# Maxima pieces around the two score steps of an attention block

## The reference

```
x = x + 0.5 * ffn(layernorm(x))     # router picks 1 of 8 experts per token: (u * silu(g)) @ w_down.T
x = x + attention(layernorm(x))
x = x + 0.5 * ffn(layernorm(x))     # the same weights again

attention: q = x @ Wq.T             # 8 heads of 64
           kv = x @ Wkv_down.T      # latent of 64, shared by the heads
           k, v = kv @ Wk_up.T, kv @ Wv_up.T
           out = softmax(q k.T / 8) v @ Wo.T
```

## Time and profile before

| | |
|---|---|
| time, median of 3 runs | 1205.15 us (1203.85 to 1205.66) |
| the profiled execution: its time | 1205.7 us |
| the profiled execution: span, first to last instruction | 1203.9 us |
| mean granted TensorE clock, as a share of 2.4 GHz | 0.92 |
| busy: PE, DVE, POOL, ACT | 984.3, 735.9, 676.9, 483.2 us |
| DVE's reductions L737 | 256, 311.9 us in sum |
| attention loop, pairs of heads | from about 240 us to 1020 us |

### The profile page before, as it was taken

The page is one execution under the profiler, slowest core; times in us unless marked ns, Lnnn a source line. Parts: engine busy times, 40 slices in busy tenths (PEclk is TensorE's granted clock), DMA queues, the critical chain, the costliest instruction groups (busy, mean ns, idle before and its releaser), DMA issues.

```text
span 1203.9 us, 17005 instructions
## 1 busy us (share of the span) xinstructions
PE 984.3 (82%) x5096; PEld 551.8 (46%) x5097; DVE 735.9 (61%) x1195; ACT 483.2 (40%) x760; POOL 676.9 (56%) x385
## 2 busy tenths in 40 slices
PE   5839975399999989999988999998999999469700
PEld 4828842144444454434454444445344555448600
DVE  6565556747677745667774677777566735555431
ACT  1253431154444434444434444442355653444300
POOL 0025452267868717768754777773587885045371
PEclk9999967599999989999999999999899999569955
DMA  8054532100000100000010000001002000145453
GB/s 292 0 171 149 146 95 91 39 1 1 1 2 1 62 1 1 1 1 1 1 62 2 1 1 1 1 1 62 1 1 106 2 1 1 63 144 162 131 151 120
DMA packets 40046, 62.22 MB, mean 52 GB/s; under 512 B 5936, under 2 KB 33072, under 8 KB 38960
## 3 DMA queue, kind: packets, MB, share of 16 engines
q1 hardware_dynamic: 20000, 27.40, 6.4%
q0 software_dynamic: 6912, 18.88, 5.8%
q10 hardware_dynamic: 13072, 15.09, 3.6%
HBM read 30.81 MB, written 23.07 MB: 45 GB/s over the span
## 4 chain that ended last, share of the span: by engine, by line
PE 63%; DVE 16%; issue 8%; ACT 5%; DMA 3%; POOL 1%; DVEq 1%; ACTq 0%; POOLq 0%; SPq 0%
PE ps_o L949 16%; PE ps L936 9%; PE ps L731 7%; PE ps L571 6%; DVE maxes L737 5%; DVE rows_store L1259 5%; PE ps_x L711 4%; PE ps L1082 3%; PE ps L208 2%; PE ps_x L970 2%; ACT rows_store L487 2%; PE ps L555 2%; PE ps_o L587 1%; PE ps_x L587 1%; PE ps L223 1%
## 5 line engine op out<-in xcount | busy, mean ns | idle before, releaser
L737 DVE TENSOR_REDUCE maxes<-ps 128x2 f32<-128x1024 f32 x256 | 311.9, 1218 | 213.9 <-PE ps L731 211.4
L1342 POOL TENSOR_TENSOR arena_b<-arena_b 128x1024 f32<-128x1024 f32 x112 | 268.3, 2396 | 164.1 <-PE ps_o L949 123.1
L1342 POOL TENSOR_TENSOR arena_b<-arena_b,hot_store 128x1024 f32<-128x1024 f32 x112 | 268.8, 2400 | 84.1 <-ACT hot_store L1140 42.1
L936 PE MATMUL ps<-q_split,keys_now 64*128 64x512 f32 x1536 | 207.2, 395 | 0.0
L1140 ACT ACTIVATE arena_b<-ps 128x1024 f32<-128x1024 f32 x144 | 144.4, 1023 | 104.3 <-PE ps L936 104.1
L520 POOL DMA_INDIRECT arena_b<-scaled_x,token_of x80 | 75.7, 947 | 179.3 <-issue 81.7
L936 PEld LDWEIGHTS ps<-q_split,keys_now 64*128 64x128 f32 x1536 | 147.5, 188 | 31.7 <-issue 2.4
L949 PE MATMUL ps_o<-arena_b,latent_now 128*64 128x512 f32 x576 | 148.9, 617 | 3.1 <-ACT arena_b L1140 0.4
L1140 ACT ACTIVATE hot_store<-ps 128x1024 f32<-128x1024 f32 x112 | 111.9, 1022 | 54.9 <-PE ps L936 54.7
L1259 DVE RECIPROCAL rows_store<-rows_store 128x256 f32<-128x256 f32 (+1 forms) x72 | 112.6, 1565 | 12.0 <-ACT rows_store L1151 12.0
L949 PE MATMUL ps_o<-hot_store,latent_now 128*64 128x512 f32 x448 | 116.6, 617 | 3.3 <-ACT hot_store L1140 0.9
(11 more groups left out here) (182 smaller groups left out, 1145.8 us busy)
## 6 DMA issues: line engine op xcount, KB each, us to landing
sorted_y<-arena_b ACTq DMA_DIRECT2D x80, 128.0 KB
scaled_x<-rows_store SPq DMA_DIRECT2D x32, 256.0 KB, 2.1
x_res<-x_in SPq DMA_DIRECT2D x4, 1024.0 KB, 13.0
keys_now<-keys_next SPq DMA_DIRECT2D x4, 1024.0 KB, 4.6
out<-x_res SPq DMA_DIRECT2D x32, 128.0 KB
arena_a<-w_gu SPq DMA_DIRECT2D x1, 2048.0 KB, 15.9
keys_max_now<-keys_max_next SPq DMA_DIRECT2D x4, 512.0 KB, 5.4
arena_a<-w_gu ACTq DMA_DIRECT2D x1, 2048.0 KB, 7.7
```

The source lines that it names most:

```text
L737: nc.vector.tensor_reduce(maxes[:, 2 * m:2 * m + 2], ps[2][:, :, :], AX_X, ALU.max) \
L936: last = nc.tensor.matmul(ps_s[n % 2][:, a, :], keys_now[h, key, k], query[h, p, q], start=False, stop=(kt >= KT - STRIDE and query is q_h ...
L1342: nc.gpsimd.tensor_tensor(t, t, prob(k, kt).rearrange("p a n -> p (a n)"), ALU.add) \
```

## The change

In a block the first piece stood ahead of both score steps, and the second behind both. Now the first stands between the two score steps. Nothing else changes: the same instructions, the same buffers.

```diff
                         after_values(p, d)
+                        scores(p, 2 * d)
                         piece()
-                        scores(p, 2 * d)
                         scores(p, 2 * d + 1)
                         piece()
```

## The result

The changed kernel takes 1265.06 us (median of 4 runs, 1264.38 to 1265.23), the kernel before beside it 1205.41 (4 runs): ratio 1.0495, 95% interval 1.0477 to 1.0514, 59.7 us slower. The forecast was 1265, +59.8. The profiled execution has a span of 1263.4, 59.5 more than before.

The account below looks back on a forecast made before the run. TensorE in program order was taken as the bound, with its waits for reductions and exponentials. Three looped batches (47.1) and the last batch (12.7) gave +59.8 us, forecast 1265 us; 8-in-10 range 1246 to 1284.

Parts of the forecast that it names:

- What holds a plain block: In plain blocks, the first piece's reduction keeps the second piece at least 1.82 us behind; the values wait for the exponential.
- the turning point: Plain block: at a reduction of 0.74 us, pieces 1.33 apart, values would start at 2.45 us, as before the change.
- The first rival: The reduction does not gate the second piece; values start 0.3 us earlier in some 90 blocks, 1178 us; chance 0.03.
- Cost of a plain block: A plain block goes from 4.37 to 4.86 us, +0.49, because the second piece waits for the reduction.
- a distance under 1.8: Declared sign of error: in a plain block the second piece comes under 1.8 us behind the first.
- The reciprocals' cover: Blocks behind a reciprocal: its delay is hidden with 0.03 us to spare, so they cost only 0.24 us each.
- Second blocks, key blocks, router blocks: Second blocks of a pair +0.69 us each, first blocks with key splits +0.92, last-batch blocks with router transposes +0.62.
- I take no change: TensorE's clock stays at the 2.4 GHz level although each longer block adds an idle 0.7 to 0.8 us.
- the second sign of being wrong: Declared sign of error: TensorE's granted clock inside the pairs falls below 0.99.
- the third rival: TensorE's clock falls in a tenth of the blocks, 12 x 3.0 = +36 us, 1301 us, open upwards; chance 0.06.
- the second rival: POOL's additions pace the last blocks of a pair, so its lag absorbs part of the loss: 1243 us; chance 0.07.
- the classes of the three looped batches: Losses by kind of block in the loop's 32 blocks per batch: 15.7 us a batch, 47.1 for three.

Follow-up runs that it names:

- experiments 1: Reductions reading 128 of 512 columns: kernel before 1174.87 us, changed kernel 1164.08 us; reading 256 columns in the changed kernel: 1188.48 us.
- experiment 2: Changed kernel with both pieces behind both score steps, nothing between the pieces: 1366.87 us, ratio 1.1332 to the kernel before.
- experiment 4: Half reciprocals cut in two around the first reduction: under the kernel before 1201.3 us (ratio 0.9974), under the changed kernel 1265.06 us (1.0503).
- experiment 3: Changed kernel with the first piece ahead of both score steps again in the six key blocks: 1252.11 us, ratio 1.0396 to the kernel before.

## Why the prediction was right

- *What holds a plain block* (two pieces apart by the reduction, values by the exponential): right, shown by experiments 1 and 2 from both sides, and for the turning point: 0.74 us was worked out, and with 0.69 the block is 4.28 against 4.37. The first rival, by which the reduction would not hold the second piece, is out.
- *Cost of a plain block*: 0.49 forecast, 0.44 measured. A piece that follows scores and not values is issued 0.80 behind the block's start, but runs 0.40 and not 0.50, and its reduction starts 0.43 to 0.45 behind it, not 0.54. So the pieces can be 1.72 apart; I had held 1.82 for their least distance, and had named a distance under 1.8 as a sign of being wrong. That sign came, and it is the hand-over that was mis-sized by 0.1, not the wait that was misread.
- *The reciprocals' cover*, called thin by 0.03: it held (experiment 4), 0.21 against 0.24 a block.
- *Second blocks, key blocks, router blocks*: 0.70, 0.93 to 0.96, 0.63 to 0.69, as worked out. Two blocks of a batch were put in a wrong class: the third of the first pair costs 0.63 and not 0.49, and the second of the last pair nothing where 0.24 was due.
- *The clock*: the step "I take no change" failed in places, and with it came the second sign of being wrong, a granted clock under 0.99 inside the pairs: it is 0.96 over each of the four with such a block (552 to 600, for one), and 1.00 from 503 to 549, in a pair without. In plain blocks the step holds (full clock with 0.65 idle in 4.83), but I did not ask it of the block with the longest wait, where two waits now stand close together. Three stretches are 1.6 above their class and one 1.15, with 0.5 more in the stretch ahead of that one: 6.5 us. That is the third rival in small, four blocks in place of twelve, at half its price. The old order in the key blocks brings the clock back (experiment 3), so the new order there is what brings the low clock about. The two waits are not the whole condition: the same ones left the clock alone in two blocks of the changed kernel, and longer ones in three of experiment 2, while the changed kernel with cut reciprocals fell in the same four as the changed one. What else it takes stays open. The Trainium skill ("TensorE: Matmul & The Clock Gate", A second HAM failure mode: psum-queue depth-cycling) says that frequent small idle times between matmul groups make the clock swing. In the plain blocks this trace does not agree (0.65 idle, clock 1.00); in the key blocks the clock does fall, though not each time.
- *POOL's lag* (the second rival): the last blocks of a pair cost 0.21 to 0.46 all the same, so they absorb none of it; what it gives back lies at the ends of the batches, as told next.

The total is closer than its parts, and that it came within 0.1 us is luck, because their errors offset each other: the classes of the three looped batches sum to 14.6 a batch and not 15.7 (-3.4), the last batch to 13.0 and not 12.7 (+0.3), the clock adds 6.5, and the stretches between two batches and ahead of the loop are 3.7 shorter than before (31.79, 30.38 and 24.86 became 30.24, 30.22 and 23.66, and 0.8 ahead). Together 47.1 - 3.4 + 13.0 + 6.5 - 3.7 = 59.5, the measured difference of the spans.

Why the stretches between batches are shorter can be read from the traces. Behind the last values of a batch the output product (L1082) waits for DVE's last multiplication L1266, before and after:

```profile
414.52 2.34 DVE L1266 TENSOR_TENSOR arena_b<-arena_b,rows_store 128x512 f32<-128x512 f32 x1
416.92 3.72 PE L1082 MATMUL ps<-w_vo,arena_b 128*128 128x256 f32 x16 [1.72 <-DVE arena_b L1266]
```

```profile
431.49 1.09 DVE L1266 TENSOR_TENSOR arena_b<-arena_b,rows_store 128x512 f32<-128x512 f32 x1
432.64 3.72 PE L1082 MATMUL ps<-w_vo,arena_b 128*128 128x256 f32 x16 [0.47 <-DVE arena_b L1266]
```

It starts 1.25 behind the values in both, but takes 1.09 in place of 2.34, and so TensorE waits 1.25 less, in each of the three places. What differs is POOL: the addition that L1266 meets there ends 3.05 behind the values before and 1.80 after, as if POOL had caught up in the longer blocks. In both kernels L1266 ends 0.55 behind the end of that addition, which fits a wait for it; no run varied POOL by itself. This gain is 3.75 in all, and the sum had no term for it. In the second of the three places 1.1 is lost again: the granted clock is low for 6.8 us there and not for 3.4. The 0.8 ahead of the loop wasn't followed up.

## What to carry to other kernels

Where one buffer is filled and drained in turn, look at the distance between the two fills in the in-order queue and compare it with fill, drain and hand-over; spreading the fills "evenly" over the work only helps if the smaller distance stays above that. A wait for something else (here the exponential) may hide that such a distance has no slack left; a block's turning point can be worked out from starts alone. And a free spot in front of a wait can be used only by work whose own inputs are ready there.

## What the runs showed of the hardware

- The reduction from PSUM took 0.424, 0.691 and 1.224 us for 256, 512 and 1024 float32 elements per partition: 1.04 ns an element and 0.16 us.
- TensorE's clock stayed at the 2.4 GHz level with 0.65 idle in each 4.83 and with 1.32 in each 5.5 of experiment 2, and with single waits of 1.3 in front of the keys. With two waits and 0.5 of work between, it fell in three of three blocks at 0.41 and 1.56, in one of three at 0.42 and 1.29, in three of three at 1.32 and 1.29 and in none of three at 1.33 and 1.56 (experiment 2).
- A multiplication of 512 float32 elements per partition on DVE with both inputs in SBUF (L1266) took 0.68 at its shortest. Where it started beside an addition of POOL (L1342) that ended before it, it took 0.73 to 2.90 and ended 0.55 behind the end of that addition, each time in both kernels.
- Score and value steps in turn take 2.14 per piece, score and value step; in the order before, the same three are 0.34 + 0.69 + 0.96 = 1.99. The order in turn changes more often between the two kinds of matmul (64 rows by 128 columns, 128 rows by 64 columns); whether that is what costs the 0.15 wasn't tried.
